# A GRU scan and a routed expert stage on one core: the input projection moved in between the recurrent matmuls

## The chip, the cores and the metric

The kernel runs on one core of a Trainium2 chip. Its time is the device time of one execution in microseconds; the median of three runs of the kernel before is 11314.01 us (11313.32 to 11315.26).

## The reference

```python
# x [4, 1024, 1024], cond [4, 1024] (the first state), all float32
def cell(h, x_t):                       # 1024 steps, one after the other
    gi = x_t @ W_ih + b_ih              # [4, 3072], needs no h
    gh = h @ W_hh + b_hh                # [4, 3072], needs the last h
    r = sigmoid(i_r + h_r); z = sigmoid(i_z + h_z)
    n = tanh(i_n + r * h_n)
    return (1 - z) * n + z * h
hs = scan(cell, cond, x)                # [4, 1024, 1024]
# routed expert stage on hs: 8 experts of rank 128, the best 2 of a softmax over logits of hs / |hs|
out = x + sum_e combine[:, e] * (hs @ Wa[e] @ Wb[e])
```

## The kernel before

Three blocks of work follow each other, each with its own instruction streams: `input_projection`, `recurrence`, `routed_ffn` (this last one is not touched).

**input_projection** computes gi for all 1024 steps. w_ih (12.6 MB, f32) stays in SBUF as [128, 8 chunks of the contraction, 3072]. Time is cut into 16 blocks of 64 steps, so a block has 4 x 64 = 256 moving columns. SP loads x of a block (16 DMAs of 64 KB, rows of 1 KB), DVE transposes it in 32x32 squares (L118), PE runs 24 output groups of 8 matmuls each, 128x128 against 256 columns, f32 (L136; each is two records in the trace), ACT adds the bias and copies each group out of PSUM (L156), SP stores a block of gi to DRAM (3 MB).

**recurrence** first splits w_hh into three bf16 parts (high, middle, low), in 16 pieces, on ACT (L397, L400) and DVE (L314, L319); PE waits for all of it. Then come the steps. The state h is split into three bf16 parts too, and these 12 columns (3 parts x 4 rows of the batch) are the stationary operand; the w_hh parts are moving. The 3072 outputs lie in four column quarters of the array (32 columns each), so four matmuls run side by side. The state is cut into PARTS: part 0 is chunks 0 to 2 and part 1 chunks 3 to 7 of 8. On the input side a part is what PE must wait for (`parts_ready[k]`), on the output side it is one PSUM bank (`ps[k]`): 288 columns for part 0, 480 for part 1. A step on PE is, in this order:

```python
pe.wait_ge(parts_ready[0], ...)
products(t, 0, 0); products(t, 0, 1)                  # 36 matmuls of 288, 36 of 480 columns
pe.wait_ge(parts_ready[1], ...)
products(t, 1, 0).then_inc(mm_done[0], 1)             # 60 of 288
products(t, 1, 1).then_inc(mm_done[1], 1)             # 60 of 480
```

DVE waits for `mm_done[k]`, transposes the bank (L332), sums the parts, adds gi, computes the gates with ACT (sigmoid L407, tanh L410) and splits the new h (L372 to L384); the last operation of a part, L384, raises `parts_ready[k]`. DVE does part 0, then part 1. SP loads gi two steps at a time (96 KB, rows of 768 B), stores h two steps at a time (32 KB), and each of the four slots of h is written again four steps later. The loop body has 4 steps.

**routed_ffn** starts when the last step is done. The change doesn't touch it, but it has a form that matters here: the router's logits (L737, L742) are f32 matmuls of 32 stationary columns in four quarters, against 128 moving columns.

Of the kernel before, what the change touches and what calls it, by code (L numbers as in the profile page):

```python
# [4 lines left out]
FP32 = mybir.dt.float32  # L5
# [5 lines left out]
P = 128  # L11
Q = 32
# [6 lines left out]

def input_projection(nc, x, w_ih, b_ih, b_hh, gi_dram):


    B, T, D = x.shape
    NC = D // P
    NM = GATES * NC
    TB = 64
    NB = T // TB  # L30
    TQ = TB // Q
    GW = D // NQ
    BANKS = 4
    with ExitStack() as ctx:
        def sb(name, shape):
            return ctx.enter_context(nc.sbuf_tensor(name, shape, FP32))

        def sem(name):
            return ctx.enter_context(nc.semaphore(name))

        w = sb("w_ih_sb", [P, NC, GATES * D])
        x_raw = [sb(f"x_raw{s}", [P, B, TQ, GW]) for s in range(2)]
        x_t = [sb(f"x_t{s}", [P, NC, B, TQ, Q]) for s in range(2)]
        stage = [sb(f"gi_stage{s}", [P, TB, NM, B]) for s in range(2)]
        bias = sb("gi_bias", [P, GATES, NC])
        bias_hh = sb("gi_bias_hh", [P, 2, NC])
        ps = [ctx.enter_context(nc.psum_tensor(f"gi_ps{n}", [P, 512], FP32)) for n in range(BANKS)]
        w_in = [sem(f"w_ih_in{q}") for q in range(GATES)]
        bias_in = sem("bias_in")
        bias_ready = sem("bias_ready")  # L50
        x_in = [sem(f"x_in{s}") for s in range(2)]
        xt_ready = sem("xt_ready")
        xt_read = [sem(f"xt_read{s}") for s in range(2)]
        mm_done = sem("gi_mm_done")
        bank_read = [sem(f"gi_bank_read{n}") for n in range(BANKS)]
        gi_out = [sem(f"gi_out{s}") for s in range(2)]
        block = ctx.enter_context(nc.Block())

        @block.sync
        def _(sp):  # L60
            def load_x(s, blk):

                for j in range(NQ):
                    for b in range(B):
                        src = x[b, bass.ds(blk * TB, TB), j * GW:(j + 1) * GW]
                        sp.dma_start(x_raw[s][j * Q:(j + 1) * Q, b, :, :],
                                     src.rearrange("(q i) f -> i q f", i=Q)).then_inc(x_in[s], DMA)

            def store_gi(s, blk, n):
                for k in range(BANKS):  # L70

                    sp.wait_ge(bank_read[k], START + (blk + 1) * (NM // BANKS))
                sp.dma_start(gi_dram[:, bass.ds(blk * TB, TB), :],
                             stage[s][:, :, :, :].rearrange("p t m b -> p t (m b)")).then_inc(gi_out[s], DMA)

            for s in range(2):
                sp.sem_inc(gi_out[s], DMA * START)
            load_x(0, 0)
            for q in range(GATES):

                for j in range(NQ):
                    sp.dma_start(w[j * Q:(j + 1) * Q, :, q * D:(q + 1) * D],
                                 w_ih[j * GW:(j + 1) * GW, q * D:(q + 1) * D].rearrange("(c i) n -> i c n", i=Q))\
                      .then_inc(w_in[q], DMA)
            load_x(1, 1)
            with sp.Fori(0, NB // 2 - 1) as n:
                for s in range(2):

                    sp.wait_ge(xt_ready, 2 * n + s + 1)
                    load_x(s, 2 * n + s + 2)  # L90
                    store_gi(s, 2 * n + s, n)
            for s in range(2):
                store_gi(s, NB - 2 + s, NB // 2 - 1)
            for s in range(2):
                sp.wait_ge(gi_out[s], DMA * (START + NB // 2))

        @block.gpsimd
        def _(pool):
            for q in range(GATES):
                pool.dma_start(bias[:, q, :], b_ih[q * D:(q + 1) * D].rearrange("(c p) -> p c", p=P),  # L100
                               allow_slow_non_contiguous=True).then_inc(bias_in, DMA)
                if q < 2:
                    pool.dma_start(bias_hh[:, q, :], b_hh[q * D:(q + 1) * D].rearrange("(c p) -> p c", p=P),
                                   allow_slow_non_contiguous=True).then_inc(bias_in, DMA)

        @block.vector
        def _(dve):
            dve.wait_ge(bias_in, DMA * (GATES + 2))
            nc.vector.tensor_tensor(bias[:, 0:2, :], bias[:, 0:2, :], bias_hh[:, :, :], ALU.add)\
              .then_inc(bias_ready, 1)  # L110
            with dve.Fori(0, NB // 2) as n:
                for s in range(2):
                    dve.wait_ge(x_in[s], (n + 1) * DMA * NQ * B)

                    dve.wait_ge(xt_read[s], START + n)
                    for b in range(B):
                        for q in range(TQ):
                            ins = nc.vector.transpose(  # L118
                                x_t[s][:, :, b, q, :],
                                x_raw[s][:, b, q, :].rearrange("p (c i) -> p c i", i=Q))  # L120
                    ins.then_inc(xt_ready, 1)

        @block.tensor
        def _(pe):
            for s in range(2):
                pe.sem_inc(xt_read[s], START)
            with pe.Fori(0, NB // 2) as n:
                for s in range(2):
                    pe.wait_ge(xt_ready, 2 * n + s + 1)
                    for m in range(NM):  # L130
                        if m % NC == 0:
                            pe.wait_ge(w_in[m // NC], DMA * NQ)

                        pe.wait_ge(bank_read[m % BANKS], START + (2 * n + s) * (NM // BANKS) + m // BANKS)
                        for c in range(NC):
                            ins = nc.tensor.matmul(  # L136
                                ps[m % BANKS][:, 0:B * TB], w[:, c, m * P:(m + 1) * P],
                                x_t[s][:, c, :, :, :].rearrange("p b q i -> p (b q i)"),
                                start=(c == 0), stop=(c == NC - 1))
                        ins.then_inc(mm_done, 1)  # L140

                    pe.wait_ge(mm_done, (2 * n + s + 1) * NM)
                    pe.sem_inc(xt_read[s], 1)  # L143

        @block.scalar
        def _(act):
            for k in range(BANKS):
                act.sem_inc(bank_read[k], START)
            act.wait_ge(bias_ready, 1)
            with act.Fori(0, NB // 2) as n:  # L150
                for s in range(2):

                    act.wait_ge(gi_out[s], DMA * (START + n))
                    for m in range(NM):
                        act.wait_ge(mm_done, (2 * n + s) * NM + m + 1)
                        nc.scalar.activation(  # L156
                            stage[s][:, :, m, :].rearrange("p t b -> p b t"),
                            ps[m % BANKS][:, 0:B * TB].rearrange("p (b t) -> p b t", b=B),
                            ACT.Identity, bias=bias[:, m // NC, m % NC:m % NC + 1])\
                          .then_inc(bank_read[m % BANKS], 1)  # L160


def recurrence(nc, h_start, w_hh, b_hh, gi_dram, hist_dram):

    T = gi_dram.shape[1]
    B, D = h_start.shape  # L170
    NC = D // P
    GW = D // NQ
    PARTS = [(0, 3), (3, NC)]
    SLOTS = 4
    CH = 2
    NI = T // SLOTS
    PW = GATES * D // 2
    PIECES = 2 * NC
    RAW = 4
    VOPS = 10  # L180
    with ExitStack() as ctx:
# [3 lines left out]
        def sem(name):  # L185
# [5 lines left out]
        gi = [sb(f"gi{s}", [P, CH, GATES, NC, B]) for s in range(2)]  # L191
# [18 lines left out]
        ps = [[ctx.enter_context(nc.psum_tensor(f"gh_ps{k}_{s}", [P, 512], FP32)) for s in range(2)]  # L210
              for k in range(2)]
        w_in = [sem(f"w_hh_in{s}") for s in range(RAW)]
# [5 lines left out]
        b_in = sem("b_cand_in")  # L218
# [580 lines left out]
```

## Time and profile before

| | us |
|---|---|
| median of three runs | 11314.01 |
| span of the profiled execution | 11311.5 |
| PE busy | 10607.6 (94%) |
| DVE busy | 5441.6 (48%) |
| ACT busy | 1706.2 (15%) |
| first recurrent matmul starts at | 1452.53 |
| last step's first DVE transpose starts at | 10357.94 |

The profiled execution's own time is its span, from the first to the last instruction; what lies around it is the 2.5 us up to the median. "Busy" is a share of time in which an engine has an instruction in flight; matmuls overlap and their ends are modelled, so a busy PE need not be the bound of a stretch. PE is TensorE, PEld its weight loads, DVE VectorE, ACT ScalarE, POOL GpSimd, SP SyncE. A name ending in q is an engine's sequencer or DMA queue.

### The profile page before, as it was taken

To read this page: it belongs to the slowest core of one execution; us is meant where nothing else is said; L and a number is where in the kernel's file an instruction comes from. 1 tells how busy PE (TensorE), PEld (TensorE's weight loads), DVE (VectorE), ACT (ScalarE), POOL (GpSimd) and SP (SyncE) were. 2 spreads that over 40 slices of the span, in tenths; PEclk is the share of its full clock that TensorE was granted. 3 is DMA by queue.
4 is the path that set the end of the run, shared out by engine and by line. 5 is a ranking of instruction groups with operands and counts; after the bars stand their busy time and mean duration, and the time that the engine had idled before them with its cause. 6 is when DMAs were issued, how large, how long until landed. Compare 5 with 4: busy or idle time off the path is not lost. (4 is left out here: it accounts for less than half of the span.)

```text
span 11311.5 us, 478913 instructions
## 1 busy us (share of the span) xinstructions
PE 10607.6 (94%) x205888; PEld 6236.8 (55%) x205888; DVE 5441.6 (48%) x29201; ACT 1706.2 (15%) x4920; POOL 27.1 (0%) x31
## 2 busy tenths in 40 slices
PE   8999889999999999999999999999999999998999
PEld 7888745555555555555555555555555555554444
DVE  0000065555555555555555555555555555554111
ACT  1222221111111111111111111111111111111111
POOL 0000000000000000000000000000000000000000
PEclk9999999999999999999999999999999999999999
DMA  3111100000000000000000000000000000001111
GB/s 86 59 45 53 66 26 7 8 7 7 7 8 7 7 7 8 7 7 8 8 7 7 8 7 7 7 8 7 7 7 8 7 7 7 8 7 59 65 45 45
DMA packets 201271, 218.57 MB, mean 19 GB/s; under 512 B 89633, under 2 KB 179745, under 8 KB 198177
## 3 DMA queue, kind: packets, MB, share of 16 engines
q1 hardware_dynamic: 201056, 218.24, 6.4%
q0 software_dynamic: 192, 0.02, 0.0%
q8 instruction: 15, 0.25, 0.0%
q14 instruction: 8, 0.06, 0.0%
HBM read 134.29 MB, written 83.89 MB: 19 GB/s over the span
## 5 line engine op out<-in xcount | busy, mean ns | idle before, releaser
L425 PE MATMUL gh_ps<-w_hh_parts,h_parts 128*12 128x288 bf16 (+1 forms) x196608 | 8349.3, 326 | 636.1 <-DVE h_parts L384 559.1
L425 PEld LDWEIGHTS gh_ps<-w_hh_parts,h_parts 128*12 128x12 bf16 x196608 | 4645.1, 88 | 4340.2 <-DVE h_parts L384 1535.4
L332 DVE STREAM_TRANSPOSE gh<-gh_ps 128x288 f32<-128x288 f32 (+1 forms) x2048 | 1192.9, 582 | 2177.9 <-PE gh_ps L425 2177.9
L407 ACT ACTIVATE gate<-pre 128x24 f32<-128x24 f32 (+1 forms) x2048 | 470.0, 229 | 6542.1 <-DVE pre L345 6542.1
L136 PE MATMUL gi_ps<-x_t,w_ih_sb 128*128 128x256 f32 x6144 | 1332.8, 380 | 42.8 <-DMA w_ih_sb<-in_L_cond_W_ih 32.7
L136 PEld LDWEIGHTS gi_ps<-x_t,w_ih_sb 128*128 128x128 f32 x6144 | 1167.8, 190 | 207.4 <-issue 48.8
L338 DVE TENSOR_REDUCE gh_sum<-gh 128x36 f32<-128x108 f32 (+1 forms) x2048 | 648.4, 317 | 71.0
L354 DVE TENSOR_TENSOR r_cand<-h_cand,gate 128x12 f32<-128x12 f32 (+1 forms) x2048 | 360.4, 176 | 612.3 <-ACT gate L407 612.3
L410 ACT ACTIVATE cand<-cand_in 128x12 f32<-128x12 f32 (+1 forms) x2048 | 441.8, 216 | 1105.2 <-DVE cand_in L357 1105.2
L118 DVE STREAM_TRANSPOSE x_t<-x_raw 128x256 f32<-128x256 f32 x128 | 43.7, 408 | 1155.9 <-PEq L143 1092.2
L366 DVE TENSOR_TENSOR zn<-one_minus_z,cand 128x12 f32<-128x12 f32 (+1 forms) x2048 | 359.9, 176 | 424.1 <-ACT cand L410 424.1
L718 PE MATMUL ps_u<-ht,wa 128*128 128x512 f32 x1024 | 449.4, 593 | 0.0
L763 PE MATMUL ps_y<-wb,us 128*128 128x512 f32 x1024 | 440.8, 592 | 0.0
L156 ACT ACTIVATE gi_stage<-gi_ps,gi_bias 128x256 f32<-128x256 f32 x384 | 269.6, 702 | 1084.8 <-PE gi_ps L136 1084.8
L379 DVE TENSOR_TENSOR h_parts<-h,h_parts 128x12 bf16<-128x12 f32 (+1 forms) x2048 | 359.7, 176 | 149.9
L345 DVE TENSOR_TENSOR pre<-gh_sum,gi 128x24 f32<-128x24 f32 (+1 forms) x2048 | 393.5, 192 | 70.8
L372 DVE TENSOR_TENSOR h_parts<-zn,zh 128x12 bf16<-128x12 f32 (+1 forms) x2048 | 358.8, 175 | 70.5
L357 DVE TENSOR_TENSOR cand_in<-r_cand,gi 128x12 f32<-128x12 f32 (+1 forms) x2048 | 357.8, 175 | 70.5
L384 DVE TENSOR_TENSOR h_parts<-h_rest,h_parts 128x12 bf16<-128x12 f32 (+1 forms) x2048 | 357.7, 175 | 69.8
L348 DVE TENSOR_TENSOR h_cand<-gh_sum,b_hh_candidate 128x12 f32<-128x12 f32 (+1 forms) x2048 | 345.2, 169 | 0.0
L374 DVE TENSOR_TENSOR h<-zn,zh 128x12 f32<-128x12 f32 (+1 forms) x2048 | 344.4, 168 | 0.0
L381 DVE TENSOR_TENSOR h_rest<-h,h_parts 128x12 f32<-128x12 f32 (+1 forms) x2048 | 344.0, 168 | 0.0
(74 smaller groups left out, 1925.1 us busy)
## 6 DMA issues: line engine op xcount, KB each, us to landing
gi_scratch<-gi_stage SPq DMA_DIRECT2D x16, 3072.0 KB, 9.8
gi<-gi_scratch SPq DMA_DIRECT2D x512, 96.0 KB, 1.9
x_raw<-in_x SPq DMA_DIRECT2D x256, 64.0 KB, 4.4
h_scratch<-h SPq DMA_DIRECT2D x512, 32.0 KB, 1.5
h_raw<-h_scratch SPq DMA_DIRECT2D x8, 2048.0 KB, 7.4
x_nat<-in_x SPq DMA_DIRECT2D x8, 2048.0 KB, 11.9
out<-y_out SPq DMA_DIRECT2D x64, 256.0 KB, 2.0
w_ih_sb<-in_L_cond_W_ih SPq DMA_DIRECT2D x12, 1024.0 KB, 33.7
```

Source lines behind the costliest of these rows:

```text
L136: ins = nc.tensor.matmul(ps[m % BANKS][:, 0:B * TB], w[:, c, m * P:(m + 1) * P], x_t[s][:, c, :, :, :].rearrange("p b q i -> p (b q i)"), ...
L332: nc.vector.transpose(gh[k][:, :, :, :], ps[k][t % 2][:, 0:GATES * n * Q].rearrange("p (q c i) -> p q c i", q=GATES, i=Q))\
L338: nc.vector.tensor_reduce(gh_sum[k][:, :, :, :].rearrange("p q c b -> p (q c) b"), gh[k][:, :, :, 0:SPLIT * B].rearrange("p q c (s b) -> p ...
L345: nc.vector.tensor_tensor(pre[k][:, :, :, :], gh_sum[k][:, 0:2, :, :], x_gates.rearrange("p q (c b) -> p q c b", b=B), ALU.add)\
L354: nc.vector.tensor_tensor(r_cand[k][:, :, :], h_cand[k][:, :, :], gate[k][:, 0, :, :], ALU.mult)\
L366: nc.vector.tensor_tensor(zn[k][:, :, :], omz[k][:, :, :], cand[k][:, :, :], ALU.mult)\
L379: nc.vector.tensor_tensor(h_parts[:, t % 2, c0:c1, 1, :], h[:, t, c0:c1, :], h_parts[:, t % 2, c0:c1, 0, :], ALU.subtract).then_inc(chain, 1)
L407: nc.scalar.activation(gate[k][:, :, :, :], pre[k][:, :, :, :], ACT.Sigmoid)\
L410: nc.scalar.activation(cand[k][:, :, :], cand_in[k][:, :, :], ACT.Tanh)\
L425: ins = nc.tensor.matmul(ps[k_out][t % 2][j * Q:j * Q + SPLIT * B, 0:GATES * (o1 - o0) * Q], h_parts[:, (t - 1) % 2, c, :, :].rearrange("p ...
L718: ins = nc.tensor.matmul(ps_u[e % KU][:, :], wa[:, e, c, :], ht[:, c, :, :].rearrange("p b t -> p (b t)"), start=(c == 0), stop=(c == NC - 1))
L763: ins = nc.tensor.matmul(ps_y[y % KY][:, :], us[:, e, b, :], wb[:, e, hf * 512:(hf + 1) * 512], start=(e == 0), stop=(e == E - 1))
```

## The change

`input_projection` is gone as a block of its own. w_ih no longer stays in SBUF: SP streams it, one output group (512 KB, rows of 512 B, four DMAs) at a time, into three slots, 24 groups for each block of 64 steps. The projection is cut into tiles: tile i is output group i // 8, contraction chunk i % 8, that is one 128x128 block of w_ih against 256 columns, issued as four matmuls of 32 stationary columns, each into its own quarter of the PSUM bank. The first block's 192 tiles run ahead of the recurrence, while ACT and DVE split w_hh (now 32 pieces, loaded through GpSimd's queue). The 192 tiles of block n+1 run within the 64 steps of block n by a fixed plan: (tiles ahead of the second part's products, tiles at the end of the step) = (0, 2) in step 0, (2, 1) in most steps, (3, 1) in seven of them, none in the last two. ACT evicts a group after the gates of the step in which its last tile was; SP stores it (128 KB). DVE transposes x of the next block in steps 0 and 1, four chunks each, ahead of the step's own work. gi lies in DRAM by group now, and is loaded for 8 steps at a time, as 24 rows of 128 B per partition; the first of these loads of a block is issued in step 62 of the block before. The loop body has 64 steps and runs 15 times; the last block has a loop of its own, of 8 or 16 steps, without tiles.

```diff
+def tile_schedule(steps, tiles):
+    extra = {5, 13, 21, 29, 37, 45, 53}
+    counts = [(0, 2)] + [(3, 1) if t in extra else (2, 1) for t in range(1, steps - 2)] + [(0, 0)] * 2
+    ...
 # SyncE
+            def load_w(m):
+                for j in range(NQ):
+                    sp.dma_start(w_i[m % WR][j * Q:(j + 1) * Q, :, :],
+                                 w_ih[j * GW:(j + 1) * GW, m * P:(m + 1) * P].rearrange("(c i) n -> i c n", i=Q))\
+                      .then_inc(w_i_in[m % WR], DMA)
+            def store_gi(f, m):
+                sp.wait_ge(gi_read, f * NM + m + 1)
+                sp.dma_start(gi_dram[:, bass.ds(f * NM + m, 1), :].rearrange("p m t -> p (m t)"), stage[m % 2][:, :])\
+                  .then_inc(gi_out[m % 2], DMA)
+            def load_gi(blk, k):
+                sp.dma_start(gi[k % 2][:, :, :, :, :].rearrange("p q c t b -> p (q c) (t b)"),
+                             gi_dram[:, bass.ds(blk * NM, NM), k * CH * B:(k + 1) * CH * B])\
+                  .then_inc(gi_in[k % 2], DMA)
...
+            load_x(0)
+            for m in range(WR):
+                load_w(m)
...
+            for m in range(NM):
+                sp.wait_ge(gi_done, m + 1)
+                load_w((m + WR) % NM)
+                if m == 0:
+                    sp.wait_ge(xt_ready, NC)
+                    load_x(1)
+                store_gi(0, m)
...
+            with sp.Fori(0, NB - 1) as n:
+                for t in range(TB):
+                    if t == 2:
+                        sp.wait_ge(xt_ready, (n + 2) * NC)
+                        load_x((n + 2) % NB)
+                    for m in ended([*PLAN[t][0], *PLAN[t][1]]):
+                        sp.wait_ge(gi_done, (n + 1) * NM + m + 1)
+                        load_w((m + WR) % NM)
+                        store_gi(n + 1, m)
+                    if t % PAIR:
+                        store_h(n, t)
+                    if t % CH == CH - 1 and t // CH + 2 < NCH:
+                        load_gi(n, t // CH + 2)
+                    if t == TB - 2:
+                        for s in range(2):
+                            sp.wait_ge(gi_out[s], (n + 2) * (DMA * NM // 2))
+                        load_gi(n + 1, 0)
+                load_gi(n + 1, 1)
 # VectorE
+            def transpose_x(f, c):
+                nc.vector.transpose(x_t[:, c, :, :].rearrange("p (q i) b -> p b q i", i=Q),
+                                    x_raw[:, :, :, c * Q:(c + 1) * Q]).then_inc(xt_ready, 1)
+            with dve.Fori(0, NB - 1) as n:
+                for t in range(TB):
+                    if t == 0:
+                        dve.wait_ge(x_in, XDMA * (n + 2))
+                        dve.wait_ge(gi_done, (n + 1) * NM)
+                    if t < 2:
+                        for c in range(t * NC // 2, (t + 1) * NC // 2):
+                            transpose_x(n + 1, c)
+                    for k in range(2):
+                        part(n * TB, t, ..., k)
 # ScalarE
+            with act.Fori(0, NB - 1) as n:
+                for t in range(TB):
+                    gates(n * TB, t)
+                    for m in ended([*PLAN[t][0], *PLAN[t][1]]):
+                        act.wait_ge(gi_done, (n + 1) * NM + m + 1)
+                        act.wait_ge(gi_out[m % 2], ((n + 1) * (NM // 2) + m // 2) * DMA)
+                        evict(n + 1, m)
 # TensorE
+            def project(tiles, f):
+                for i in tiles:
+                    m, c = i // NC, i % NC
+                    if c == 0:
+                        pe.wait_ge(w_i_in[m % WR], (f * (NM // WR) + (m // WR + 1)) * (DMA * NQ))
+                        if not (m < 2 and isinstance(f, int)):
+                            pe.wait_ge(gi_read, f * NM + (m - 1))
+                    if m == 0:
+                        pe.wait_ge(xt_ready, f * NC + (c + 1))
+                    for j in range(NQ):
+                        ins = nc.tensor.matmul(
+                            ps_i[m % 2][j * Q:(j + 1) * Q, 0:COLS], w_i[m % WR][:, c, j * Q:(j + 1) * Q],
+                            x_t[:, c, :, :].rearrange("p t b -> p (t b)"),
+                            start=(c == 0), stop=(c == NC - 1))
+                    if c == NC - 1:
+                        ins.then_inc(gi_done, 1)
+            project(range(TILES), 0)
+            pe.wait_ge(cleared, 4)
+            pe.wait_ge(w_low, PIECES)
+            def step(first, t, f, plan):
+                pe.wait_ge(parts_ready[0], first + (t + 1))
+                products(t, 0, 0)
+                products(t, 0, 1)
+                project(plan[0], f)
+                pe.wait_ge(parts_ready[1], first + (t + 1))
+                products(t, 1, 0).then_inc(mm_done[0], 1)
+                products(t, 1, 1).then_inc(mm_done[1], 1)
+                project(plan[1], f)
```

## Rows read from the trace of the kernel before

**Rows 1.** The page: busy time of the engines, and PE's clock in 40 slices.

```profile
PE 10607.6 (94%) x205888; PEld 6236.8 (55%) x205888; DVE 5441.6 (48%) x29201; ACT 1706.2 (15%) x4920; POOL 27.1 (0%) x31
PEclk9999999999999999999999999999999999999999
```

**Rows 2.** Windows: busy per engine, PE's granted clock, DMA share, GB/s.

```profile
100.00:1386.00 1286.00, 1265.52 (x5846) 1109.00 (x5844) 38.49 (x113) 265.92 (x373) 0.01 (x1) 1.00 0.15 50
1386.00:1450.00 64.00, 0.00 (x0) 0.00 (x0) 56.31 (x46) 45.33 (x32) 0.87 (x1) 0.50 0.61 200
```

**Rows 3.** Timeline: start, duration, engine; first recurrent matmul, first, second and last step.

```profile
1452.53 10.54 PE L425 MATMUL gh_ps<-w_hh_parts,h_parts 128*12 128x288 bf16 x192 [76.94 <-DVE w_hh_parts L319]
1460.08 0.48 DVE L332 STREAM_TRANSPOSE gh<-gh_ps 128x288 f32<-128x288 f32 x1 [7.90 <-PE gh_ps L425]
1468.78 0.48 DVE L332 STREAM_TRANSPOSE gh<-gh_ps 128x288 f32<-128x288 f32 x1 [2.12 <-PE gh_ps L425]
...
10357.94 0.48 DVE L332 STREAM_TRANSPOSE gh<-gh_ps 128x288 f32<-128x288 f32 x1 [2.12 <-PE gh_ps L425]
```

**Rows 4.** Timeline of one step; in brackets the idle time before, and its releaser.

```profile
5008.79 0.48 DVE L332 STREAM_TRANSPOSE gh<-gh_ps 128x288 f32<-128x288 f32 x1 [2.12 <-PE gh_ps L425]
...
5011.93 3.10 PE L425 MATMUL gh_ps<-w_hh_parts,h_parts 128*12 128x288 bf16 x72 [0.16 <-DVE h_parts L384]
...
5013.95 0.22 ACT L410 ACTIVATE cand<-cand_in 128x20 f32<-128x20 f32 x1 [0.55 <-DVE cand_in L357]
...
5015.42 5.05 PE L425 MATMUL gh_ps<-w_hh_parts,h_parts 128*12 128x288 bf16 x120 [0.39 <-DVE h_parts L384]
```

**Rows 5.** Groups by form: busy us, mean ns of one, idle before and releaser.

```profile
L425 PE MATMUL gh_ps<-w_hh_parts,h_parts 128*12 128x480 bf16 x98304 | 5334.0, 366 | 0.0
L425 PE MATMUL gh_ps<-w_hh_parts,h_parts 128*12 128x288 bf16 x98304 | 3371.3, 286 | 636.1 <-DVE h_parts L384 559.1 <-DVE w_hh_parts L319 76.9
```

**Rows 6.** Timeline of two evictions of the projection.

```profile
1310.01 0.70 ACT L156 ACTIVATE gi_stage<-gi_ps,gi_bias 128x256 f32<-128x256 f32 x1 [2.75 <-PE gi_ps L136]
1313.47 0.70 ACT L156 ACTIVATE gi_stage<-gi_ps,gi_bias 128x256 f32<-128x256 f32 x1 [2.75 <-PE gi_ps L136]
```

**Rows 7.** The router's products: timeline, and the loads' ns min/median/max.

```profile
10500.23 1.95 PE L737 MATMUL ps_logits<-ht,router 128*32 128x128 f32 x64
10502.00 1.93 PE L742 MATMUL ps_logits<-hsq,one_col 128*32 128x128 f32 x64
...
L737 PEld LDWEIGHTS ps_logits<-ht,router x512: 106/110/177, 10382.7 to 11194.3; 128*32 128x32 f32 x171
```

**Rows 8.** Timeline of PE: a bf16 matmul between f32 ones.

```profile
10409.57 0.38 PE L729 MATMUL ps_b<-comb_t,sel 128*128 128x512 bf16 x1
10409.79 7.03 PE L718 MATMUL ps_u<-ht,wa 128*128 128x512 f32 x16
```

**Rows 9.** Timeline of ACT: the table load of the loop.

```profile
5005.57 1.28 ACT L407 ACT_TABLE_LOAD   x1
```

**Rows 10.** The start: x's transposes, and windows as in rows 2.

```profile
13.00 2.73 DVE L118 STREAM_TRANSPOSE x_t<-x_raw 128x256 f32<-128x256 f32 x8 [1.72 <-DMA x_raw<-in_x]
...
0.00:8.00 8.00, 0.00 (x0) 0.00 (x0) 0.00 (x0) 0.00 (x0) 4.76 (x9) 1.00 0.72 84
24.00:32.00 8.00, 0.00 (x0) 0.00 (x0) 0.00 (x0) 0.00 (x0) 0.00 (x0) 1.00 1.03 212
1395.00:1405.00 10.00, 0.00 (x0) 0.00 (x0) 8.89 (x6) 9.59 (x8) 0.00 (x0) 0.50 0.93 345
```

**Rows 11.** The DMA queue from 1500 to 10360: packets, MB, share of 16 engines.

```profile
q1 hardware_dynamic: 146448, 66.68, 2.9%
```

**Rows 12.** PE's instruction pages (whole span; 1461 to 1470), and gi loads (us to landing).

```profile
q8 instruction: 15, 0.25, 0.0%
q8 instruction: 2, 0.03, 1.7%
gi<-gi_scratch SPq DMA_DIRECT2D x512, 96.0 KB, 1.9
```

More of the change, by code:

```diff
@@ L17, with recurrence @@
 SPLIT = 3
-def input_projection(nc, x, w_ih, b_ih, b_hh, gi_dram):
+def tile_schedule(steps, tiles):
+    extra = {5, 13, 21, 29, 37, 45, 53}
+    counts = [(0, 2)] + [(3, 1) if t in extra else (2, 1) for t in range(1, steps - 2)] + [(0, 0)] * 2
+    assert sum(a + b for a, b in counts) == tiles
+    at, plan = 0, []
+    for a, b in counts:
+        plan.append((range(at, at + a), range(at + a, at + a + b)))
+        at += a + b
+    return plan
+def recurrence(nc, x, h_start, w_ih, w_hh, b_ih, b_hh, gi_dram, hist_dram):
     B, T, D = x.shape
@@ L28, in input_projection @@
     NM = GATES * NC
+    GW = D // NQ
     TB = 64
@@ L31, in input_projection @@
     TQ = TB // Q
[L32 to L160, printed above, removed]
@@ L163, in recurrence @@
[L163 to L172, printed above, removed]
+    COLS = TB * B
+    TILES = NM * NC
+    PLAN = tile_schedule(TB, TILES)
     PARTS = [(0, 3), (3, NC)]
     SLOTS = 4
[L175 to L178, printed above, removed]
+    PAIR = 2
+    CH = 8
+    NCH = TB // CH
+    PW = GATES * D // 4
+    PIECES = 4 * NC
     RAW = 4
     VOPS = 10
+    WR = 3
+    XDMA = DMA * NQ * B
@@ new lines, in last_block @@
+            def last_block(i, more):
+                for t in range(2 * CH):
+                    if t % PAIR:
+                        store_h(NB - 1, t, i * (2 * CH))
+                    if t % CH == CH - 1 and more:
+                        k = t // CH
+                        sp.dma_start(gi[k][:, :, :, :, :].rearrange("p q c t b -> p (q c) (t b)"),
+                                     gi_dram[:, (NB - 1) * NM:NB * NM, bass.ds((i + 1) * (2 * CH * B) + k * CH * B, CH * B)])\
+                          .then_inc(gi_in[k], DMA)
@@ new lines, in _ @@
+            with sp.Fori(0, NCH // 2 - 1) as i:
+                last_block(i, True)
+            last_block(NCH // 2 - 1, False)
+            for s in range(2):
+                sp.wait_ge(hist_out[s], DMA * (START + T // PAIR // 2))
+            sp.wait_ge(x_in, XDMA * (NB + 1))
+            for s in range(WR):
+                sp.wait_ge(w_i_in[s], DMA * NQ * (NB * (NM // WR) + 1))
+        @block.gpsimd
+        def _(pool):
+            for q in range(GATES):
+                pool.dma_start(bias[:, q, :], b_ih[q * D:(q + 1) * D].rearrange("(c p) -> p c", p=P),
+                               allow_slow_non_contiguous=True).then_inc(bias_in, DMA)
+                if q < 2:
+                    pool.dma_start(bias_hh[:, q, :], b_hh[q * D:(q + 1) * D].rearrange("(c p) -> p c", p=P),
+                                   allow_slow_non_contiguous=True).then_inc(bias_in, DMA)
+            pool.dma_start(b_cand[:, :], b_hh[2 * D:3 * D].rearrange("(c p) -> p c", p=P),
+                           allow_slow_non_contiguous=True).then_inc(b_in, DMA)
@@ L273, in _ @@
[L273 to L283 removed]
+                    pool.wait_ge(w_high, n - RAW + 1)
@@ L289, in _ @@
+            for c in range(NC):
+                transpose_x(0, c)
+            dve.wait_ge(bias_in, DMA * (GATES + 2))
+            nc.vector.tensor_tensor(bias[:, 0:2, :], bias[:, 0:2, :], bias_hh[:, :, :], ALU.add)\
+              .then_inc(bias_ready, 1)
             for k in range(2):
@@ L320, in _, with part @@
                                             ALU.subtract).then_inc(w_low, 1)
-            def part(i, t, k):
+            dve.wait_ge(b_in, DMA)
+            def part(first, t, chunks, hists, k):
                 c0, c1 = PARTS[k]
                 n = c1 - c0
-                x_gates = gi[t // CH][:, t % CH, 0:2, c0:c1, :].rearrange("p q c b -> p q (c b)")
-                x_cand = gi[t // CH][:, t % CH, 2, c0:c1, :]
-                step = SLOTS * i + t
+                s = t // CH % 2
+                x_gates = gi[s][:, 0:2, c0:c1, t % CH, :]
+                x_cand = gi[s][:, 2, c0:c1, t % CH, :]
+                now, last, sp_ = t % SLOTS, (t - 1) % SLOTS, t % 2
+                step = first + t
                 links = (2 * step + k) * VOPS
@@ L383, in part @@
+                nc.vector.tensor_tensor(h_rest[k][:, :, :], h[:, now, c0:c1, :],
+                                        h_parts[:, sp_, c0:c1, 0, :], ALU.subtract).then_inc(chain, 1)
                 dve.wait_ge(chain, links + 10)
[L384 to L390 removed]
+                nc.vector.tensor_tensor(h_parts[:, sp_, c0:c1, 2, :], h_rest[k][:, :, :],
+                                        h_parts[:, sp_, c0:c1, 1, :], ALU.subtract).then_inc(parts_ready[k], 1)
@@ L392, in _, with evict @@
+            with dve.Fori(0, NCH // 2) as i:
+                for t in range(2 * CH):
+                    for k in range(2):
+                        part(i * (2 * CH) + (NB - 1) * TB, t, i + (NB - 1) * (NCH // 2),
+                             i * (2 * CH // SLOTS) + (NB - 1) * (TB // SLOTS) + t // SLOTS, k)
         @block.scalar
         def _(act):
+            def evict(f, m):
+                nc.scalar.activation(stage[m % 2][:, :], ps_i[m % 2][:, 0:COLS], ACT.Identity,
+                                     bias=bias[:, m // NC, m % NC:m % NC + 1]).then_inc(gi_read, 1)
```

143 lines of the change are left out of this document (74 added, 69 removed).

## The prediction

> **What bounds the kernel now.** I read the page first: the span is 11311.5 us, PE is busy 94% of it and at full granted clock in every slice [rows 1]. Next the stretches: a projection of some 1375 us in which PE alone works, a hole of about 77 us in which PE does nothing (DVE and ACT split w_hh into three bf16 parts, up to the first recurrent matmul at 1452.53), 1024 recurrent steps, and the expert stage [rows 2, 3]. The DVE marks of the first and the last step, 1460.08 and 10357.94, are 1023 steps apart: 8.698 us a step [rows 3].
>
> "94% busy" doesn't tell whether a step is bound by PE, so the timeline of one step decides. Call D the start of the 288-wide DVE transpose, at 5008.79. PE restarts at D+3.14 (5011.93, first h part ready) and at D+6.63 (5015.42, second part ready), and the next D comes at D+8.70, 2.07 us after the second restart [rows 3, 4]. What ends PE's wait at each restart is the last DVE operation, L384, of a part [rows 4]. So the loop is one chain: 15 quads of PE, the DVE chain of part 0, the DVE chain of part 1. PE has slack in it, DVE none but the 2.12 us in which it waits for PE.
>
> How much slack? A step is 96 matmuls of 288 columns and 96 of 480, which run four at a time in column quarters: 24 x 120 ns + 24 x 200 ns = 7.68 us at 2.4 GHz. From the start of the 120 matmuls at 5015.42 to the start of their last one is 5.05 - 0.366 = 4.68 us, where 15 x 0.120 + 14 x 0.200 = 4.60: about 3 ns more per quad. A step of PE work is then 48 x 0.163 = 7.83 us, and 0.87 us of each step is free: 0.32 after the last products, 0.55 ahead of the second part. The idle 559.1 us that the row shows (0.55 a step) is smaller because the last matmul of each run is drawn 0.37 long [rows 4, 5].
>
> **The change, part by part.** *Removed:* everything from 0 to 1452.5 us in its present form. The rest of the sum is built up anew.
>
> (a) *One tile.* A tile is one 128x128 block of w_ih against 256 columns. In the old form a group of 8 takes 3.455 us (evictions at 1310.01 and 1313.47), 0.432 a tile [rows 6]. In quarters it issues four times as many loads and matmuls (each f32 matmul is two records). Nearest row: the router's products, f32, 32 columns, 128 moving: 64 matmuls and 64 loads of about 110 ns in 10502.00 - 10500.23 = 1.77 us, so 8 quads at 0.221, where four passes of 128 columns are 0.213 [rows 7]. So quarters do run side by side in f32, with the loads beneath, and a tile of 256 columns is 0.427 + 0.008 = 0.435 us. Bounds: 0.427 and, loads fully exposed, 0.85. I take 0.435.
>
> (b) *A step with tiles.* Most steps get two tiles ahead of the second part and one at the end. PE ends the step's last products at D+2.82; the tile takes it to D+3.25, 0.12 past the moment at which part 0 is ready. Products of part 0: 9 x 0.123 + 9 x 0.203 = 2.93, to D+6.19; two tiles, to D+7.05, while part 1 is ready at D+6.63. Then 2.07 as before: 9.12 us, bound by PE, DVE now 0.42 early. The tiles are hidden to 0.87 of 1.30 us only. A block of 64 steps: 64 x 7.83 + 192 x 0.435 + two steps without tiles (2 x 0.87 idle) = 501.1 + 83.5 + 1.7 = 586.3 us, against 556.7. Fifteen blocks: 8794.
>
> (c) *Seams* between bf16 and f32 matmuls. In the expert stage a bf16 matmul between f32 ones takes 0.22 us start to start (10409.57 to 10409.79), which is its 512 columns, so nothing is lost [rows 8]. In quarters and next to waits with register arithmetic no row shows it; bounds 0 to 0.1 us a step, I take 0.03 x 915 = 27 us.
>
> (d) *Evictions*, 24 a block of 0.70 us on ACT, are queued behind the second tanh of the step (D+5.2) and end near D+6; the next sigmoid is wanted at D+9.12+1.0. Even two table loads of 1.28 us around each would fit [rows 4, 6, 9]. *Transposes of x*: 4 ahead of each of steps 0 and 1, 0.34 us each (8 in 2.73), 1.37 us inside the 2.12 us in which DVE waits for PE [rows 4, 10]. If they took twice that, 0.6 us x 30 = 18 us. Cost 0.
>
> (e) *DMA in the recurrence.* Per block: 24 x 512 KB of w_ih, 1 MB of x, 3 MB of gi out and in, the last as 3072 packets of 128 B per load of 8 steps. Packets of 256 to 768 B cost 0.029 x 8860 x 16 / 146448 = 28 ns now; those of x into 32 partitions cost 0.72 x 8 x 16 / 656 = 140 ns [rows 10, 11]. So a gi load takes 5 to 27 us, hidden where it is issued 8 steps ahead. Only the first load of a block is issued late: after the last tile's store, at about 8.5 us past D of step 61, and wanted some 27 us past it. SP's queue holds the store of h behind x's 16 issues (5 us) and behind the waits for tiles, but the h slots are wanted back two steps later. Cost 0, up to 8 us a block.
>
> (f) *Instruction fetch.* The body grows from 4 to 64 steps, 64 x 384 + 192 x 16 = 27,648 loads and matmuls on PE. Now the body is fetched once: pages of some 17 KB (0.25 MB in 15) arrive in the first steps (two between 1461 and 1470, about 1.2 us each) and none after 1500, where the queue of the data is the only one [rows 11, 12]. That the steps with arriving pages also take 8.70 us (1460.08 to 1468.78) shows that fetching in sequence is hidden at a page per 5 to 6 us [rows 3]. What isn't shown is the jump back. Estimate: one small DMA's landing (1.9 us) plus a page's 0.9 [rows 12]: 14 x 2.8 = 39 us, bounds 0 and, three engines one after another, 118.
> The Trainium skill has a rule against this change (Runtime: NRT & Kernel Launch, "Instruction fetch mechanics"): the fetch buffer prefetches only forward, and a taken branch to a page outside it stalls until that page has come. No run here shows its price yet; by that rule the 64-step body pays once a block, and the sum would move by the same tens of microseconds.
>
> (g) *The start.* PE needs x (its transposes started at 13.00 before) and one tile of w_ih; 24 groups are then 83.5 us of PE, to about 102. The w_hh splitting runs beside it instead of behind it: DVE was busy 56 us in that hole. What comes last is DMA: w_ih moved at 212 GB/s in 4 KB rows, x in 1 KB rows at 84/0.72 = 117; w_hh at 345 [rows 2, 10]. With w_ih now in 512 B rows, 12.6 MB takes 60 us at the first rate and 108 at the second (the nearer row); w_hh adds up to 36, gi and x some 15. First recurrent matmul: at best 115, at worst 190; I take 150.
>
> (h) *Last block and tail*: unchanged. 63 steps of 8.698 = 548, and from the last D 11311.5 - 10357.9 = 953.6.
>
> Sum: 150 + 7.6 (first matmul to first D, at half clock) + 8794 + 548 + 953.6 = 10453; with fetch 39 and seams 27: 10519. The median of the runs is 2.5 us above the profiled span, so 10522, about 10520: 7.0% less than now.
>
> **Rivals.** *Loads exposed (the other side).* All quarters contract over the same 128 rows; if a load waits for the matmuls in flight, a tile costs its 8 loads of 106 ns besides or in place of the streaming: 0.85 us. Then 15 x 192 x 0.415 = 1195 us more: 11,715. It decides from a tile of (11311.5 - 10519)/2880 + 0.435 = 0.71 us. Against it: 0.221 per quad with the same loads [rows 7]. Chance 0.04.
> The Trainium skill says (TensorE: Matmul & The Clock Gate, "Packing small matmuls") that loads overlap running matmuls only when the row group differs, which would give this rival; the trace disagrees, with 64 loads and 64 matmuls of one row group in 1.77 us.
>
> *Seams cost.* Four changes between kinds a step, with PE's queue drained by waits: at 0.05 us each 0.2 a step, 183 us in place of 27: 10,680. For it: no row shows the two kinds in turns in quarters, with waits between. Against it: PE runs 0.4 us behind, so the waits are over when it comes to them, and the one turn of kinds that a row shows is free [rows 8]. Chance 0.16.
>
> *The turn of the block.* gi's first chunk lands late (27 us, the upper bound of (e)) and engines refetch: 10 us x 15 = 150 in place of 39: 10,630. Chance 0.08.
>
> *The tiles cost nothing* (the step stays at 8.70): 15 x 29.6 = 444 less, 10,080. It needs PE to have 1.30 us of room where 0.87 are free. Chance 0.02.
>
> **How the numbers follow.** Forecast 0.70, within 10,400 (start 115, no seams, no fetch cost) and 10,650. The two middle rivals reach to 10,750; I take 10,400 to 10,750. About 0.2% (23 us) is what a measurement can tell: faster 0.95, same 0.01, slower 0.04.
>
> **What would show it.** Steps of 9.12 us between D marks with tiles, 8.70 in the last block; DVE's wait for PE grown from 2.12 to about 2.5; PE's wait for h parts gone in steps with tiles. Eight tiles in a row at the start, 3.47 us between evictions where loads keep up. First recurrent matmul between 115 and 190 us; a gap of 1 to 5 us in PE once per block; PE instruction pages through the whole recurrence. The forecast is wrong if a tile takes over 0.5 us, if steps exceed 9.3, or if pages arrive too late in straight flow.

## The result and the profile after

The changed kernel takes 10520.74 us (median of 4 runs, 10517.0 to 10528.88), the kernel before beside it 11313.79: a ratio of 0.930 (95% interval 0.9286 to 0.9313). The prediction was 10520, range 10400 to 10750. The profiled execution is the longest of the four, with a span of 10527.1.

By the marks D (start of the 288-wide transpose), the 784.4 us of difference between the spans [rows 3] are: first D at 150.07 instead of 1460.08, -1310.0; the 1023 steps in 9423.8 instead of 8897.9, +525.9; from the last D to the end 953.2 instead of 953.6. So the whole gain lies in what no longer stands ahead of the steps, and 40% of it is given back in them.

The page after, with two queues that fetch instructions, PE's (q8) and a second one (q14), beside [rows 1, 12]; then the groups by form, beside [rows 5]:

```profile
PE 10330.0 (98%) x224296; PEld 5969.7 (57%) x224320; DVE 5471.8 (52%) x29233; ACT 1279.3 (12%) x4704; POOL 44.3 (0%) x63
...
q8 instruction: 1774, 29.07, 1.1%
...
q14 instruction: 586, 4.80, 0.2%
```

```profile
L437 PE MATMUL gh_ps<-w_hh_parts,h_parts 128*12 128x288 bf16 x98304 | 3377.3, 286 | 121.2 <-DVE h_parts L362 61.0 <-issue 57.6
...
L456 PEld LDWEIGHTS gi_ps<-x_t,w_ih_tile 128*32 128x32 f32 x24576 | 741.5, 111 | 637.9 <-DMA w_ih_tile<-in_L_cond_W_ih 56.3 <-issue 10.4
...
L311 DVE STREAM_TRANSPOSE gh<-gh_ps 128x288 f32<-128x288 f32 x1024 | 494.2, 483 | 2530.5 <-PE gh_ps L437 2530.5
```

PE's wait for h has fallen from 559.1 to 61.0 us, and DVE's wait for PE has grown from 2177.9 to 2530.5: the bound of a step has moved from the h chain to PE, as the run with half the columns confirms below. One step in the timeline (start, duration, engine), beside [rows 4]:

```profile
5005.53 0.48 DVE L311 STREAM_TRANSPOSE gh<-gh_ps 128x288 f32<-128x288 f32 x1 [2.45 <-PE gh_ps L437]
...
5008.34 0.60 PE L456 MATMUL gi_ps<-x_t,w_ih_tile 128*32 128x256 f32 x8
...
5008.77 3.10 PE L437 MATMUL gh_ps<-w_hh_parts,h_parts 128*12 128x288 bf16 x72
...
5011.69 1.04 PE L456 MATMUL gi_ps<-x_t,w_ih_tile 128*32 128x256 f32 x16
...
5012.56 5.05 PE L437 MATMUL gh_ps<-w_hh_parts,h_parts 128*12 128x288 bf16 x120
...
5014.62 0.48 DVE L311 STREAM_TRANSPOSE gh<-gh_ps 128x288 f32<-128x288 f32 x1 [2.52 <-PE gh_ps L437]
```

Read the starts: the tile at the end of the step begins at D+2.81 and takes 0.43, part 0's products 2.92, two tiles 0.87, and D follows 2.06 later: 9.09 us, and no PE row has an idle time before it. Over the whole run 690 of the 1023 intervals are 9.1 us and 110 are 9.5 (105 steps have a fourth tile).

Two places are not as in steady flow. The turn of the 64-step loop (the timeline around one; "issue" is an engine waiting for nothing that the profile shows):

```profile
1324.49 0.48 DVE L311 STREAM_TRANSPOSE gh<-gh_ps 128x288 f32<-128x288 f32 x1 [2.12 <-PE gh_ps L437]
...
1329.83 7.99 PE L437 MATMUL gh_ps<-w_hh_parts,h_parts 128*12 128x288 bf16 x192 [2.36 <-issue]
...
1332.59 1.28 ACT L408 ACT_TABLE_LOAD   x1 [2.72 <-issue]
1334.11 2.05 DVE L255 STREAM_TRANSPOSE x_t<-x_raw 128x256 f32<-128x256 f32 x4 [3.05 <-issue]
1336.00 0.45 DVE L311 STREAM_TRANSPOSE gh<-gh_ps 128x288 f32<-128x288 f32 x1
```

Each of the three engines stalls at its own jump back; from D to D it is 11.51 where 8.70 would be. The last row has no idle time in front of it: DVE comes late from its jump, has x's transposes to do first (2.05 us), and the next D starts right behind them. It is so in 12 of the 14 turns. The last block's PE loop has 8 steps, and turns seven times:

```profile
9122.63 0.48 DVE L311 STREAM_TRANSPOSE gh<-gh_ps 128x288 f32<-128x288 f32 x1 [2.12 <-PE gh_ps L437]
...
9127.68 1.91 PE L437 MATMUL gh_ps<-w_hh_parts,h_parts 128*12 128x288 bf16 x29 [2.06 <-issue]
...
9130.46 9.19 PE L437 MATMUL gh_ps<-w_hh_parts,h_parts 128*12 128x288 bf16 x163 [0.87 <-issue]
9136.66 0.48 DVE L311 STREAM_TRANSPOSE gh<-gh_ps 128x288 f32<-128x288 f32 x1 [7.46 <-PE gh_ps L437]
```

Here PE stops twice, the second time after 29 matmuls, and from D to D it is 14.0 us. After the stops PE also runs at the lower of its two clock levels. In this window, as in [rows 2], the 0.50 ahead of the DMA share and the GB/s is the granted clock, so 1.2 GHz in place of 2.4:

```profile
9132.00:9133.00 1.00, 1.00 (x16) 0.66 (x12) 0.00 (x0) 0.00 (x0) 0.00 (x0) 0.50 1.17 134
```

The granted clock falls so in each of these seven turns, and in 7 of the 14 turns of the 64-step loop.

The start, and the share of 16 engines that the data queues took from 0 to 150 us:

```profile
150.07 0.48 DVE L311 STREAM_TRANSPOSE gh<-gh_ps 128x288 f32<-128x288 f32 x1 [2.70 <-PE gh_ps L437]
...
157.80 0.18 DVE L324 TENSOR_TENSOR pre<-gh_sum,gi 128x24 f32<-128x24 f32 x1 [6.93 <-DMA gi<-gi_scratch]
...
160.13 5.22 PE L437 MATMUL gh_ps<-w_hh_parts,h_parts 128*12 128x288 bf16 x72 [6.20 <-DVE h_parts L362]
```

```profile
q1 hardware_dynamic: 35512, 19.41, 63.4%
q0 software_dynamic: 2752, 12.61, 31.2%
```

The two queues take 95% of the 16 engines' time over the whole of it. The first step waits 6.9 us for gi, which can only be loaded once the last of the 24 groups is stored; behind that wait the granted clock is 0.50 again, and part 0's 72 products take 5.22 us instead of 3.10.

### The profile page after: what moved, and what is told of

It reads as the page before. It is cut to its first block and busy times, and to the rows that moved or that the text cites. A ratio compares the mean times of both kernels' runs of the same rounds, so it can differ in the third digit from the quotient of the medians.

```text
span 10527.1 us, 516114 instructions
## 1 busy us (share of the span) xinstructions
PE 10330.0 (98%) x224296; PEld 5969.7 (57%) x224320; DVE 5471.8 (52%) x29233; ACT 1279.3 (12%) x4704; POOL 44.3 (0%) x63
## 5 line engine op out<-in xcount | busy, mean ns | idle before, releaser
L437 PEld LDWEIGHTS gh_ps<-w_hh_parts,h_parts 128*12 128x12 bf16 x196608 | 4804.5, 88 | 3392.5 <-DVE h_parts L362 380.8
L311 DVE STREAM_TRANSPOSE gh<-gh_ps 128x288 f32<-128x288 f32 (+1 forms) x2048 | 1192.5, 582 | 2530.5 <-PE gh_ps L437 2530.5
L456 PE MATMUL gi_ps<-x_t,w_ih_tile 128*32 128x256 f32 x24576 | 1658.3, 381 | 49.6 <-DMA w_ih_tile<-in_L_cond_W_ih 49.6
L456 PEld LDWEIGHTS gi_ps<-x_t,w_ih_tile 128*32 128x32 f32 x24576 | 741.5, 111 | 637.9 <-DMA w_ih_tile<-in_L_cond_W_ih 56.3
L339 DVE TENSOR_TENSOR zh<-gate,h 128x12 f32<-128x12 f32 (+1 forms) x2048 | 346.4, 169 | 1.2
L337 DVE TENSOR_SCALAR one_minus_z<-gate 128x12 f32<-128x12 f32 (+1 forms) x2048 | 343.7, 168 | 1.9
```

The source lines that it names most:

```text
L311: nc.vector.transpose(gh[k][:, :, :, :], ps[k][sp_][:, 0:GATES * n * Q].rearrange("p (q c i) -> p q c i", q=GATES, i=Q))\
L437: ins = nc.tensor.matmul(ps[k_out][t % 2][j * Q:j * Q + SPLIT * B, 0:GATES * (o1 - o0) * Q], h_parts[:, (t - 1) % 2, c, :, :].rearrange("p ...
L456: ins = nc.tensor.matmul(ps_i[m % 2][j * Q:(j + 1) * Q, 0:COLS], w_i[m % WR][:, c, j * Q:(j + 1) * Q], x_t[:, c, :, :].rearrange("p t b -> ...
```

## The experiments

All are edits of the changed kernel, except the two of the old one.

**Half the columns.** Is it PE's streaming that made the step longer?

```diff
-    ps_i[m % 2][j * Q:(j + 1) * Q, 0:COLS], ..., x_t[:, c, :, :]
+    ps_i[m % 2][j * Q:(j + 1) * Q, half * COLS // 2:(half + 1) * COLS // 2], ...,
+    x_t[:, c, half * TB // 2:(half + 1) * TB // 2, :]        # half = c // 4
```

> Each tile streams only 128 of its 256 columns (chunks 0 to 3 do the first half of the bank, 4 to 7 the second), so half of the projection's products are left out; every load, matmul, wait and DMA stays. If PE's streaming bounds the step and the h chain (8.70 us) lies just beneath it, a tile takes 0.22 us, PE needs 7.83 + 0.65 = 8.48 and the steps fall back to 8.70 from 9.09: 15 x (54 x 0.39 + 7 x 0.83) = 403 us less, about 10,115. If the step had grown by the number of instructions or by the change between bf16 and f32, it stays at 9.09 and the time at 10,520.

Measured: 10146.45 us. In the timeline PE's loads wait for h ahead of both parts, 0.21 and 0.30 us:

```profile
5007.07 0.48 DVE L311 STREAM_TRANSPOSE gh<-gh_ps 128x288 f32<-128x288 f32 x1 [2.12 <-PE gh_ps L437]
...
5010.21 2.62 PEld L437 LDWEIGHTS gh_ps<-w_hh_parts,h_parts 128*12 128x12 bf16 x72 [0.21 <-DVE h_parts L362]
...
5013.78 4.57 PEld L437 LDWEIGHTS gh_ps<-w_hh_parts,h_parts 128*12 128x12 bf16 x120 [0.30 <-DVE h_parts L362]
```

Of the 1023 intervals 634 are 8.7: with the same number of instructions, seams, waits and DMAs the step falls back to the chain. The growth was streaming. The 31 us above the forecast lie in the intervals of 8.8 to 9.1; the old kernel with a long DVE body, below, has much the same ones (63 us over 8.70 a step here, 55 there, turns left out).

**Tiles in one piece.** What do the quarters buy?

```diff
-    for j in range(NQ): matmul(ps_i[m % 2][j * Q:(j + 1) * Q, 0:COLS], w_i[m % WR][:, c, j * Q:(j + 1) * Q], ...)
+    matmul(ps_i[m % 2][:, 0:COLS], w_i[m % WR][:, c, :], ...)
```

> The tiles as one matmul of 128 stationary columns in place of four of 32. Streaming alone gives 0.432 us a tile and the same step of 9.09: 10,520. If a change between the array in four column quarters and the array in one piece costs PE its drain (0.09 us between the router's last quarter matmul and the first full one in the kernel before, perhaps up to the 0.17 us by which a matmul outlasts its columns), four changes a step cost 915 x 4 x 0.09 to 0.17 = 330 to 620 us: 10,850 to 11,140. The Trainium skill states that rule (TensorEngine Tiling (Array Packing), Key Properties: a change of mode, not of tile, drains the engine). I expect the second.

Measured: 11051.78 us, 531 more. PE in one step:

```profile
5004.27 0.48 DVE L311 STREAM_TRANSPOSE gh<-gh_ps 128x288 f32<-128x288 f32 x1 [3.12 <-PE gh_ps L437]
...
5007.18 0.30 PEld L455 LDWEIGHTS gi_ps<-x_t,w_ih_tile 128*128 128x128 f32 x2 [0.41 <-issue]
5007.18 0.70 PE L455 MATMUL gi_ps<-x_t,w_ih_tile 128*128 128x256 f32 x2
...
5007.81 2.62 PEld L437 LDWEIGHTS gh_ps<-w_hh_parts,h_parts 128*12 128x12 bf16 x72 [0.33 <-issue]
...
5007.81 3.10 PE L437 MATMUL gh_ps<-w_hh_parts,h_parts 128*12 128x288 bf16 x72
...
5010.84 1.13 PE L455 MATMUL gi_ps<-x_t,w_ih_tile 128*128 128x256 f32 x4
5011.90 5.05 PE L437 MATMUL gh_ps<-w_hh_parts,h_parts 128*12 128x288 bf16 x120
```

Against the quarters' step, the first full-width tile of a run starts 0.10 us late (D+2.91 for D+2.81; 3.03 for 2.92), and from there to the products behind it is 0.20 more (0.63 for 0.43; 1.06 for 0.87): 0.61 a step, two thirds of the gain. It is the change of the array's division, not of the type, that costs, since the type changes in both kernels. The loads' rows show two parts. At each change the load starts together with the first matmul behind it, whereas within one division it starts some 0.2 us before, beneath the matmuls ahead: in the changed kernel the tile's loads begin at 5008.14 and its matmuls at 5008.34. So PE stands for 0.09 us at each change, both ways (0.296 and 0.309 us from start to start, for 0.20 and 0.216 otherwise), and the first full-width load is no longer hidden (0.32 us to the second matmul, for 0.216). The forecast had a drain of 0.09 to 0.17 at four changes; the measured sum is about 4 x 0.09 and twice 0.10 for the loads, and it fell into the range with a part that the forecast didn't have.

**All tiles ahead of the second part.** Does the place of a tile matter?

```diff
-    for a, b in counts:
+    for a, b in [(a + b, 0) for a, b in counts]:
```

> All tiles of a step ahead of the second part's products, none at its end. If the two gaps of PE are filled one by one, PE idles 0.3 us ahead of the first part again, and three tiles end at D+3.14+2.93+1.30 = D+7.37, so D to D is 7.37+2.07 = 9.44: 15 x 61 x 0.35 = 320 us more, about 10,840. If only PE's sum of work counts, wherever the tiles stand, it stays at 10,520.

Measured: 10877.31 us.

```profile
5012.30 0.48 DVE L311 STREAM_TRANSPOSE gh<-gh_ps 128x288 f32<-128x288 f32 x1 [2.89 <-PE gh_ps L437]
...
5015.45 3.10 PE L437 MATMUL gh_ps<-w_hh_parts,h_parts 128*12 128x288 bf16 x72 [0.17 <-DVE h_parts L362]
5018.38 1.47 PE L456 MATMUL gi_ps<-x_t,w_ih_tile 128*32 128x256 f32 x24
```

Part 0's products start at D+3.15, as before the change; tiles at D+6.08, and with 1.29 for three and 2.07 the step is 9.44, as forecast. The step before this one, from 5002.54 to 5012.30, is 9.76: there a short DVE stall of 0.23 falls into part 0's chain, which has no slack in this kernel. Such steps aren't the reason for the 37 us above the forecast, though: outside the turns the steps take 324 us more than in the changed kernel, where 320 were forecast. The rest lies in the 14 turns, 31 us together (14.06 us on average, for 11.84). This edit also moves step 0's two tiles ahead of the second part, and there they wait for x's transposes, behind DVE's jump:

```profile
1373.34 2.07 DVE L255 STREAM_TRANSPOSE x_t<-x_raw 128x256 f32<-128x256 f32 x4 [3.21 <-issue]
1374.11 1.07 PE L456 MATMUL gi_ps<-x_t,w_ih_tile 128*32 128x256 f32 x16 [2.41 <-DVE x_t L255]
```

**The last block's loop.** What is the price of a turn?

```diff
-    with pe.Fori(0, NCH) as i:
-        for t in range(CH):
-            step(i * CH + (NB - 1) * TB, t, None, ((), ()))
+    with pe.Fori(0, 2 * NCH) as i:                    # body of 4 steps
+        for t in range(CH // 2):
+            step(i * (CH // 2) + (NB - 1) * TB, t, None, ((), ()))
```

> The last block's PE loop with a body of 4 steps (16 passes) in place of 8 steps (8 passes). The changed kernel's D marks show 13.7 to 14.5 us instead of 8.7 at each of 7 turns of that loop, 37 us in all. If the price is that the jump's target has left the fetch buffer, the body of 4 steps (1536 loads and matmuls, as in the kernel before) stays in it and no turn costs: 10,484. If each turn of a loop costs by itself, 15 turns cost 80 us: 10,563.

Measured: 10487.86 us (10483.15 to 10490.14).

```diff
+    for t in range(TB):                               # or: no loop at all
+        step((NB - 1) * TB, t, None, ((), ()))
```

> The last block's 64 steps on PE written out, no loop. If straight flow is fetched for nothing and only the backward jump costs, the 7 turns' 37 us go as in the variant with 4 steps: 10,484. If fetching itself costs wherever pages are new, it stays near 10,520.

Measured: 10483.33 us (10482.09 to 10486.94). From the first D to the end of the span the two take 10341.8 and 10343.2 us, the changed kernel 10377.0: 35 and 34 less, and the last block alone 34 less in both (554.1 for 588.4). The seven turns were 37 over 8.70 a step; three of them fall on turns of DVE's own loop, which stay and cost 0.9 to 1.2 each in these two runs. Twice as many turns of a body of 1536 loads and matmuls cost nothing, as they would if it stays in PE's instruction buffer, and new pages in straight flow cost PE nothing. In both runs the granted clock no longer falls in the last block. Both kernels beat the changed one (0.9268 and 0.9269 of the old time, intervals 0.9255 to 0.928 and 0.9257 to 0.9282).

**The old kernel with bodies of 64 steps.** This measures instruction supply without the change.

```diff
-    with dve.Fori(0, NI) as i:
-        for t in range(SLOTS):
-            for k in range(2): part(i, t, k)
+    with dve.Fori(0, NI // 16) as i:
+        for t in range(16 * SLOTS):
+            for k in range(2): part(i * 16 + t // SLOTS, t % SLOTS, k)
```

> The kernel before, with DVE's recurrent loop written out to 64 steps a pass in place of 4, nothing else. In the changed kernel DVE shows some 200 short idle times of 0.2 to 0.5 us between its operations (52 us in all), at places that come back in each pass, and 3.0 to 3.4 us at each jump back. If they belong to DVE's instruction supply for a body that doesn't stay in its buffer, they appear here too, unhidden, since the h chain sets the step: 16 x 13.5 x 0.26 = 55 us, and 15 jumps of 3.2 us of which 2.12 lie in DVE's wait for PE, 16 us: about 11,385. If they come from the tiles, DMA or PE, this kernel takes the old time.

Measured: 11383.28 us beside 11312.43, ratio 1.0063 (1.0049 to 1.0076): 55 us in the steps, as forecast, and 11 in the 15 turns, where 16 were expected. DVE's waits for its own results, absent from the kernel before, are there (us in total, times, longest):

```profile
DVE h_parts L379 <- DVE h L374: 20.4, 63, 0.5
DVE cand_in L357 <- DVE r_cand L354: 13.6, 47, 0.3
DVE h_parts L384 <- DVE h_rest L381: 7.7, 32, 0.3
DVE h_parts L372 <- DVE zn L366: 4.7, 16, 0.3
```

With PE's and ACT's loops written out too:

> The kernel before, with the recurrent loops of PE, DVE and ACT written out to 64 steps a pass. It has the instruction supply of the changed kernel without its tiles. 15 jumps of 3.1 us (as the changed kernel's marks show, 11.8 in place of 8.7) make 46 us, DVE's short stalls 55: about 11,415. If the price at the changed kernel's block turns was not the jump but the late gi, the x transposes or the queue, little of the 46 appears.

Measured: 11413.98 us, ratio 1.009 (1.0075 to 1.0106). The 15 turns take 10.00 to 12.02 us from D to D, for 8.70, 43 us in all, and the short stalls 54. This kernel has no tiles, no x to transpose and gi in its old place, so a turn of a body of 64 steps costs by itself, and the late gi and SP's queue are out as its cause. So 102 us is the price of the 64-step bodies where the chain is the bound. Two of its turns show what the price is made of:

```profile
2016.16 9.65 PE L425 MATMUL gh_ps<-w_hh_parts,h_parts 128*12 128x288 bf16 x192 [2.37 <-issue]
...
2022.82 0.48 DVE L332 STREAM_TRANSPOSE gh<-gh_ps 128x288 f32<-128x288 f32 x1 [5.44 <-PE gh_ps L425]
```

```profile
2018.00:2019.00 1.00, 1.00 (x20) 0.48 (x12) 0.00 (x0) 0.32 (x1) 0.00 (x0) 0.50 0.11 20
```

```profile
5395.96 7.98 PE L425 MATMUL gh_ps<-w_hh_parts,h_parts 128*12 128x288 bf16 x192 [2.32 <-issue]
5400.95 0.48 DVE L332 STREAM_TRANSPOSE gh<-gh_ps 128x288 f32<-128x288 f32 x1 [3.72 <-PE gh_ps L425]
```

PE stops for 2.3 to 2.4 us in both. In the second the granted clock stays at 2.4 GHz, and D follows 4.99 us after PE's new start; in the first it falls to 1.2 GHz behind the stop, and D follows after 6.66. The clock fell in 12 of the 15 turns, about 20 of the 43 us; the other half is PE's stop itself, some 1.5 us a turn.

The changed kernel pays some 64 us of the price by its marks: 44 in its 14 turns and 20 in 107 steps of 9.2 to 9.4 in place of 9.1. The 0.4 us that DVE is early there hides most of its short stalls, which take 59 us in all. Its turns are as long as those of the old kernel, but not made the same. By the same 4.99 us, PE's stops alone would make 21 of the 44 (an estimate from PE's new starts at D+5.01 to D+5.53). The rest is the lower clock in 7 of the 14 turns and, in 12 of the 14, DVE's late return with x's transposes behind it; where both occur, they end within 0.2 us of each other, and no run separates them.

**The start.** The queue's order, or the bytes?

```diff
-    if m == 0: (wait for x's transposes) load_x(1)
+    if m == 20: ...
```

> SP issues the second block's x (16 DMAs, 7.5 us of issue) behind output group 20 of the first block instead of behind group 0. In the changed kernel PE waits 10.5 us for w_ih at 36 to 47 us, while SP issues x. If the queue's order is what it waits for, the first recurrent matmul comes at 135 instead of 145 and the time is 10,510. If the DMA engines' work as a whole bounds the start, the same bytes have to pass anyway and nothing is gained: 145, 10,520. I expect 3 to 10 us less.

Measured: 10522.07 us: nothing gained, where 3 to 10 us were expected. First D at 142.21; three executions with the changed kernel's own start have it at 139.57, 142.02 and 150.07, which is also why single spans scatter by 10 us.

```diff
-    load_w((m + WR) % NM)
+    load_w((m + WR) % NM, 1)                          # first block: chunk 0 of 8 only
```

> In the first block the reloads of w_ih bring one of eight chunks only (the first block's projection is computed from stale weights); the number of DMAs and all waits stay. If the DMA engines bound the start, PE is freed: 19 + 83.5 us of tiles and a few for the last pieces, first recurrent matmul at 105 to 112 and the time 10,480 to 10,490. If the split of w_hh on ACT and DVE paces it (it took 58 us alone before), or the issue on SP, it stays above 135.

Measured: 10495.14 us, first recurrent matmul at 114.67, somewhat above the forecast.

> Both edits at the start together: one chunk of eight in the first block's reloads of w_ih (stale weights in the first block) and x of the second block issued behind group 20. With the small loads alone PE began the steps at 114.7 and had one wait left, 8.1 us at 35 to 43, while SP issued x. If queue order is what costs once the DMA engines have room, that wait goes: first recurrent matmul at 104 to 107, the time 8 us below that of the small loads alone, about 10,487. If x's place in the queue never matters, 114 as before.

Measured: 10490.78 us, 4.4 below the small loads alone where 8 were forecast. PE's waits up to 125 us (total, times, longest):

```profile
PE gi_ps L456 <- DMA w_ih_tile<-in_L_cond_W_ih: 19.8, 1, 19.8
PE gh_ps L437 <- DVE w_hh_parts L295: 5.9, 1, 5.9
```

The tiles ran through from 28.91 to 105.1 and then w_hh's last piece was 5.9 us late: the recurrent matmuls began at 111.02 and missed the forecast of 104 to 107; only the tiles kept to it. The bytes bound the start as it is; the order of the queue counts only once they don't.

## Why the prediction was right, point by point

The terms, for the span of 10519 that was forecast and the 10527.1 measured:

- *A tile, 0.435 us*: 0.43. Loads beneath the matmuls, as the router's row said. The Trainium skill's rule that loads overlap running matmuls only where the row group differs (TensorE: Matmul & The Clock Gate, "Packing small matmuls") is contradicted here too: 111 ns loads of one row group, none exposed.
- *A step of 9.12*: 9.09, and 9.53 with a fourth tile. Both gaps were filled as reckoned; half columns and tiles ahead confirm the two gaps one by one. The 3 ns a quad were slightly too much. The other steps (no turn, not the first) took 9142 us where 9150 were reckoned.
- *Seams, 27 us*: none within quarters. At full width they would have been 0.61 a step; the rival "seams cost" (0.05 each) would have been right, threefold, for that form. The Trainium skill states the drain (TensorEngine Tiling (Array Packing), Key Properties) without a price; these runs give it.
- *Turns of the block, 39 us*: 44 (14 at 3.1). The estimate of 2.8 from a landing and a page came near to PE's stop as such (2.0 to 2.5 us idle), but such a stop alone lengthens a turn by only some 1.5; what brings the sum to 44 are two things that the prediction didn't reckon, the lower clock behind the stop and x's transposes behind DVE's jump. The size was hit by luck. The Trainium skill's rule on taken branches (Runtime: NRT & Kernel Launch, "Instruction fetch mechanics") agrees with the runs; the variant with 4 steps, whose turns are free, shows it.
- *Transposes of x, cost 0*, step (d): 0.51 us each (4 in 2.05), not the 0.34 that were taken from [rows 10]. In step 1 they still fit into DVE's wait for PE; in step 0 they stand behind DVE's jump, and D waits for them.
- *The last block "unchanged"*: wrong by 37 us in turns. Step (h) overlooked that its PE loop has 8 steps, 3072 loads and matmuls, and so leaves the buffer as well.
- *Fetching in sequence is hidden*, step (f): right for PE, wrong for DVE, which has short stalls that go with the fetching of its pages (55 us in the old kernel with a long DVE body; the last section has the count). The first steps of the old kernel couldn't show it, since they have few pages of DVE. In the changed kernel most of the price is hidden.
- *DMA in the recurrence, 0*: held at the block turns, no PE or DVE wait for gi or w_ih after the first step. Step (e) didn't look at the first block, where gi came 6.9 us late; the first interval was 18.04, 8.9 over, the other 2 through the lower clock behind that wait.
- *Start at 150 (115 to 190)*: 145.08, for the reason given, DMA. First D 7.5 earlier than the sum had it: 4.9 by the start, and 2.6 because the way from the first matmul to D took 4.99 in place of the 7.6 "at half clock". PE came to it from tiles, not from a pause of 77 us, and its granted clock was 1.00.

In sum -7.5 (start), +8.9 (first gi), +5 (turns), +37 (last block), -35 (steps and seams), -0.4: 8 us. The hit to the microsecond is luck; terms of 37, 35 and 9 us cancelled, and the 39 for the turns came near for other reasons than its own. The mechanism, a step of 8.70 by the chain and 9.1 by PE, is shown.

## What to carry to other kernels

Before moving independent work into a dependent loop, reckon the bounding engine's free time gap by gap from start-to-start distances, not from busy shares: here 0.87 us of a step were free where busy and idle showed 0.55, and the work has to be laid in each gap (0.35 us a step lost when one was left empty). Give the moved matmuls the same division of the array as those around them. After unrolling, count each loop's instructions: a body that no longer stays in its buffer costs about 3 us a turn here and short stalls on DVE, and a small residual loop can cost more per turn than a large one. Look at the granted clock behind each stop, and don't lay work that others wait for right behind a jump.

## What the runs showed that was not expected

- A loop of 8 steps on PE costs 5.3 us a turn (4.9 by the runs without it), one of 64 steps 3.1. By the marks the 37 us of its seven turns are about 10 for PE's first stop, 13 for a second one and 14 mainly for the lower clock behind them (an estimate). The second stop comes after 29 matmuls in all seven; that the jump's target lies near the end of a page would explain it, but no run moved the target, so this stays open.
- DVE, in a body that doesn't stay in its buffer, stalls 0.2 to 0.5 us at places that come back in each pass, some 15 per 64 steps. In the old kernel with the long DVE body, a packet of the instruction queue q14 starts within 1 us (mostly 0.6 to 0.9) behind 253 of 254 such stalls, where some 14 would be so by chance; in the kernel before, that queue brings nothing from 1500 to 10360 us. So each stall goes with the fetching of a page. Why it lasts 0.25 us, and why other pages come without one, stays open.
- In the loads at the start a packet of SP's queue took 0.634 x 150 x 16 / 35512 = 43 ns on average, and one of w_ih's 512 B rows 40 ns. An engine's rate on these is about 13 GB/s, that of the 4 KB rows before (212 GB/s over 16): the short rows cost much less than the 140 ns feared from x.
